# Linear attention beside a routed transformer block: in the last chunk, state products and values ahead of the third projection unit, and the order of ScalarE's work around them

## The reference, cut to what matters

```python
xn = layernorm(x)                                   # 2048 x 512
# branch 1: linear attention with decay, 16 heads of 32
q, k, v, u = split(xn @ W_qkvu.T); q, k = silu(q), silu(k)
# per head: o_t = sum over s <= t of exp(-slope (t - s)) (q_t . k_s) v_s, by blocks with a carried state
o = o * rsqrt(mean(o * o) + 1e-6);  y1 = (u * o) @ W_out.T
# branch 2: a block for the 256 tokens of highest score only (2048 // 8)
idx = sort(top_k(xn @ w_router, 256));  xs = xn[idx]
h = rms_norm(xs, ln1);  q, k, v = h @ wq + bq, h @ wk + bk, h @ wv + bv   # 16, 8, 8 heads of 128
att = softmax(causal(rope(q) @ rope(k).T / sqrt(128))) @ v
x1 = xs + att @ wo;  h2 = rms_norm(x1, ln2)
mlp = silu(h2 @ w_gate) * (h2 @ w_up) @ w_down
gate = sigmoid(sel_scores)
y2 = xn;  y2[idx] = gate * (x1 + mlp) + (1 - gate) * xs
out = x + y1 + y2
```

## Time and profile before

| | us |
|---|---|
| median of three runs | 479.21 |
| lowest and highest run | 478.12, 479.49 |
| the profiled execution, its own time | 481.46 |
| its span, first to last instruction | 479.6 |
| TensorE (PE) busy in the span | 465.2 (97%) |
| VectorE (DVE) | 298.8 (62%) |
| ScalarE (ACT) | 229.5 (48%) |
| GpSimd (POOL) | 192.2 (40%) |

### The profile page before, as it was taken

One profiled execution on the slowest core, in us unless ns is written; L12 is line 12 of the kernel. 1 busy time (PEld: TensorE's weight loads), 2 busy tenths in 40 slices (PEclk: granted clock), 3 DMA queues, 4 the chain that ended last, 5 costly groups with the idle time before them and its releaser, 6 DMA issues. The chain is left out here.

```text
span 479.6 us, 11902 instructions
## 1 busy us (share of the span) xinstructions
PE 465.2 (97%) x4839; PEld 422.3 (88%) x4839; DVE 298.8 (62%) x638; ACT 229.5 (48%) x400; POOL 192.2 (40%) x193
## 2 busy tenths in 40 slices
PE   7999999999999999999999998999999999999994
PEld 7988899998998989989899877998888878999993
DVE  6689676887499999755456856767553436230221
ACT  5951243322276779322443436565666446544430
POOL 3240251111120232041367957360470424689862
PEclk9999999999999999999999998999999999999999
DMA  7967675333522111132731689775557822555403
GB/s 227 398 146 123 121 163 85 105 107 110 167 78 68 58 58 55 47 96 65 260 133 46 220 297 326 223 252 176 182 187 274 254 94 88 160 180 186 156 1 44
DMA packets 40951, 72.14 MB, mean 150 GB/s; under 512 B 5872, under 2 KB 7424, under 8 KB 40768
## 3 DMA queue, kind: packets, MB, share of 16 engines
q1 hardware_dynamic: 40352, 70.06, 47.8%
q0 software_dynamic: 544, 1.31, 1.5%
HBM read 54.03 MB, written 17.32 MB: 149 GB/s over the span
## 5 line engine op out<-in xcount | busy, mean ns | idle before, releaser
L1178 POOL TENSOR_TENSOR wlo<-raw,whi 128x512 fp32r<-128x512 f32 x96 | 124.6, 1330 | 88.5 <-ACT whi L564 88.5
L1252 PE MATMUL banks<-HTh,whi 128*128 128x256 f32 x224 | 65.1, 290 | 0.5 <-DVE rope L922 0.4
L1254 PE MATMUL banks<-HTh,wlo 128*128 128x256 f32 x224 | 63.4, 283 | 0.0
L1253 PE MATMUL banks<-HTl,whi 128*128 128x256 f32 x224 | 63.3, 283 | 0.0
L842 DVE TENSOR_TENSOR A<-banks,DEC 128x512 f32<-128x512 f32 x64 | 39.7, 684 | 29.8 <-PE banks L1325 28.3
L1157 POOL TENSOR_TENSOR state_dec<-state,small 128x128 f32<-128x128 f32 x16 | 8.4, 527 | 114.9 <-DVE state L853 114.9
L564 ACT ACTIVATE whi<-raw 128x2048 fp32r<-128x2048 f32 x24 | 45.8, 1908 | 13.2 <-PE banks L1254 7.2
L1252 PEld LDWEIGHTS banks<-HTh,whi 128*128 128x128 f32 x224 | 42.9, 191 | 2.2 <-issue 1.7
L1253 PEld LDWEIGHTS banks<-HTl,whi 128*128 128x128 f32 x224 | 42.9, 192 | 0.3
L1254 PEld LDWEIGHTS banks<-HTh,wlo 128*128 128x128 f32 x224 | 42.9, 191 | 0.0
L1305 PE MATMUL banks<-xTh,WUh 128*128 128x256 f32 x128 | 37.6, 294 | 0.3 <-DVE WUl L787 0.3
(11 more groups left out here) (242 smaller groups left out, 1282.6 us busy)
## 6 DMA issues: line engine op xcount, KB each, us to landing
X<-in_x SPq DMA_DIRECT2D x16, 256.0 KB, 5.8
xn_all<-XN SPq DMA_DIRECT2D x16, 256.0 KB, 6.9
uo_all<-park_h SPq DMA_DIRECT2D x16, 256.0 KB, 2.3
uo_all<-park_l SPq DMA_DIRECT2D x16, 256.0 KB, 3.0
raw<-in_wq SPq DMA_DIRECT2D x4, 1024.0 KB, 6.8
uoh<-uo_all SPq DMA_DIRECT2D x16, 256.0 KB, 3.0
uol<-uo_all SPq DMA_DIRECT2D x16, 256.0 KB, 3.5
XR<-in_x SPq DMA_DIRECT2D x16, 256.0 KB, 3.6
```

Of the source, the lines that this page charges most:

```text
L1178: ins = Q.tensor_tensor(low[:, k, :], raw[b % 3][:, k, :], high[:, k, :].bitcast(f32), ALU.subtract)
L1252: T.matmul(dst, lh, rh, start=first, stop=False)
L1253: T.matmul(dst, lh, rl, start=False, stop=False)
L1254: return T.matmul(dst, ll, rh, start=False, stop=last)
```

## The change

It moves calls; none is added or removed. On TensorE `attend(15)` goes from behind unit 6 and `rms(14)` to ahead of unit 6. On ScalarE, in chunk 15, `base(0)` and `base(1)` (before: in steps h = 0 and h = 1 of the second part) come ahead of the chunk's `Square`; the gate's exponential (before: behind `unit_values(7)`) comes behind `uo_high(15)`; then `mean_square(14)` and `block_hi(5)` follow, which before stood ahead of the `Square`. The code of VectorE, GpSimd and the DMA queue is as it was.

```diff
@@ scalar engine, chunks
+            def base(N):
+
+                act.wait_ge(xr_in[N % NXR], 16 * (N // NXR + 1)), act.wait_ge(gains_ok, 1)
+                S.activation(XR[N % NXR][:], XR[N % NXR][:], ACT.Identity, scale=gain[:, N:N + 1],
+                             bias=shift[:, N:N + 1]).then_inc(base_ok, 1)
...
                 in_position(N, 2, tiles)
-                if N >= N_TILES - CH:
+                if N == N_TILES - 2:
                     mean_square(N - 1)
                 if N == N_TILES - 1:
-                    block_hi(5)
+                    base(0)
+                    base(1)
...
                     S.activation(sq[:], sums, ACT.Square).then_inc(sq_ok, 1)
                     uo_high(N)
+                if N == N_TILES - 1:
+                    act.wait_ge(sel_ok, NS)
+                    S.activation(gate, sel_score, ACT.Exp, scale=-1.0).then_inc(gate_exp, 1)
+                    mean_square(N - 1)
+                    block_hi(5)
                 count_marks(ranked(N, 2))
                 in_position(N, 3, tiles)
...
-            act.wait_ge(sel_ok, NS)
-            S.activation(gate, sel_score, ACT.Exp, scale=-1.0).then_inc(gate_exp, 1)
...
-                if h in out_at:
+                if out_at.get(h, 0) > 1:
                     base(out_at[h])
@@ tensor engine, chunks
+                if N == N_TILES - 1:
+                    attend(N)
                 in_position(N, 2)
                 if N >= N_TILES - CH:
                     rms(N - 1)
-                attend(N)
                 if N < N_TILES - 1:
+                    attend(N)
                     new_keys_values(N)
                 in_position(N, 3)
```

## The result

| | before | after |
|---|---|---|
| median of 6 runs each | 479.31 | 474.95 |
| lowest and highest | 477.99, 480.72 | 474.24, 475.87 |
| ratio, 95% interval | | 0.9907 (0.989 to 0.9925) |
| profiled execution, its own time | 481.46 | 474.24 |
| its span | 479.6 | 472.4 |

The median is 474.95 us, where 474.8 was predicted: 4.36 us faster. A second measurement of it on another chip gave 474.67 us (6 runs) against 478.37 for the kernel before (ratio 0.992, 0.9904 to 0.9937).

A forecast was written before the change was run, and what follows sets the result against it. TensorE, busy for 97% of the span, was taken to bound the kernel; 0.99 + 1.80 + 1.57 = 4.36 us off a median of 479.21 gave 474.8 us, range 473.8 to 477.2.

The forecast's parts named there:

- Which wait matters, and what holds it: TensorE's 1.8 us wait ahead of `project_out(1)` for `final(0)`, through a chain hanging on block 5's late weights.
- First term: Unit 8 on TensorE starts 0.99 us earlier, as `unit_values(7)` directly follows `block_hi(5)`, itself still at 283.57.
- The new stop ahead of unit 8: TensorE would reach unit 8 before ScalarE's values are ready and stand still for 0.4 to 1.0 us.
- attend "by itself is worth nothing": Moving attend ahead of unit 6 gains nothing alone, since unit 8 waits for ScalarE; it only enables the other part.
- Second term: The whole TensorE stop ahead of `project_out(1)` goes, since `final(0)` is done earlier: 1.80 us.
- Third term: The slow granted clock behind the stop, over 293 to 297 us, goes with the stop: 1.57 us.
- rival A: Clock gain missing from the median: runs before mostly lack the slow stretch, or the new stop brings one; 476.4 us, chance 0.13.
- Who must keep up: VectorE's `stage(8)` frees unit 9's bank with 0.3 us slack; ScalarE and the queue also keep pace.
- rival D: Slower: the chain grows again at block 6, landing late and holding `project_out(2)`; 481 us or more, chance 0.03.
- rival C: Time won at 300 us does not arrive, as feed-forward weight blocks through ScalarE and GpSimd set the pace; about 479 us, chance 0.05.
- mean_square(14): On ScalarE, moved behind the gate's exponential, it ends at 279.9, 1.5 us before head 0's scores need it.

The follow-up runs named there:

- the nudge: Kernel before plus 32 small identity matmuls, results unused, between unit 5 and unit 6, attend staying behind unit 6: 478.0 us, ratio 0.9984.

## Why the prediction was right, and where three of its steps were not

*Which wait matters, and what holds it: right.* The stop ahead of `project_out(1)` went, by cutting the chain that hung on block 5. Loading block 5 first, with no engine's order changed, removes the same stop.

*First term, unit 8, 0.99: mis-sized, measured 1.64 in the first trace of the changed kernel and 1.68 in the second.* The step that failed reads "So `block_hi(5)` again runs from 283.57". The producer of `park_l` indeed did not move (its store begins at z + 9.5 in both), but the issue behind it became 0.9 us shorter. With the load in its old place, `block_hi(5)` starts at z + 15.56 to 16.18 in the five traces with the early attend (mean 15.81) and at z + 16.13 to 16.63 in the five with the late one (mean 16.47; the nudge not counted): 0.66 us. How much of it comes from the shorter issue stays open, for the nudge had that and its block landed at z + 16.52.

*The new stop ahead of unit 8, 0.4 to 1.0 us: not there.* It is 0.1 us or less (0.56 from head 1's scores to unit 8, 0.46 in the second trace, where 0.47 is normal). TensorE arrived when calculated (17.95 against 17.83 from z); the values were earlier, for the same reason.

*attend "by itself is worth nothing": wrong.* Alone it gives about 1 us (in its trace block 5 came 0.9 us earlier), and taking it out of the changed kernel costs 1.3. The other effect I had (head 0's scores earlier, 0.42 calculated, 0.59 measured) and called hidden; with ScalarE's chain cut, TensorE sets the pace there and it counts.

*Second term, the stop, 1.80: right,* 3.51 - 1.64 = 1.87.

*Third term, the clock, 1.57: right in the trace, too large for the median.* In the profiled pair it is 5.13 - 3.51 = 1.62. But 28 of 47 executions before do not have it, to judge by their mean clock, and among those the median is 478.47. I took one trace for all of them; the first half of rival A, to which I gave 0.13, is what happened in this term. Against the executions without the slow stretch the changed kernel's 474.73 (12 runs) is a gain of 3.7 us, close to the 3.5 us by `project_out(1)`; what is above that comes from the slow ones.

So the sum of 4.36 met the measured 4.36 by chance to the extent of 0.7 us: 0.65 too little in the first term and 0.07 in the second, and 0.72 too much in the third (4.36 less the 3.51 of the first two leaves 0.85 for the clock).

*Who must keep up: right.* `stage(8)` began at the end of unit 8 and TensorE found unit 9's bank free. Block 6 was there when ScalarE got to it (285.33, no bracket), so rival D found nothing. From the transposes of h = 2 to the end pass 179.55 us before and 179.30 after: nothing was given back (rival C).

*mean_square(14)* ended at 278.05, 1.4 us ahead of head 0's scores; 1.5 was calculated.

## What to carry to other kernels

Where a chain on an engine that is mostly idle holds the busy one, look for the transfer at its head, and put in front of the wait for it all that does not need it; or issue the transfer earlier. Several small edits on one chain do not add up: moving two bases of 0.8 us each was worth 2.5 us alone and 0.2 to 0.4 on top. And a slow clock behind a stop in one trace is a price times a frequency: the times of many executions, sorted by their mean clock, give an idea of how often it is paid.

## What the runs showed of the hardware that I had not expected

- A stop of TensorE of 1.75 us was followed by a clock of 0.57 of full in one trace of the kernel before and by 1.00 in the other; 19 of 47 executions of it show the lower mean clock, and they are 1.5 us slower. With the stop filled, gone or cut to 0.23 us no execution of 58 had a mean of 0.994 or less, against 17 of 55 with it.
- The issue of the store of `park_l` (256 KB) took the queue engine 0.43 us in seven traces and 1.18 to 1.68 us in six. In all six long ones a packet of 0.02 MB on the instruction queue starts at z + 9.7 or 9.8, just ahead of the issue (z + 9.9); in all seven short ones it has passed by z + 8.5.
- The order of work on TensorE so reached the issue of a transfer with which it shares no data: moving attend, or putting 32 unused matmuls in its place, moved the packet and shortened the issue. That the packet carries TensorE's instructions fits this and was not tested by itself.
